# Edge scores by one matmul over two float parts, one-hots on ScalarE, and message weights in PSUM

## The chip, the cores and the metric

The kernel runs as one program on 1 core of one Trainium2 chip. The metric is the device time of an execution in microseconds (us); where kernels are compared, runs of both on the same chip are used.

## What is computed

A graph attention layer, a mixture of experts, a graph transformer layer and again a mixture of experts, over 2500 nodes with 256 features and 80000 edges that are sorted by destination. The part that matters here is in each graph layer. Layer 0 has H = 4 heads and no self loops, layer 1 has H = 8 heads and a self loop at every node.

```python
# layer 0 (H = 4): e_s and e_d are scores of nodes, h the nodes' values
scores = leaky_relu(e_s[src] + e_d[dst], 0.2)
m = segment_max(scores, dst)
ex = exp(scores - m[dst])
alpha = ex / segment_sum(ex, dst)[dst]
agg = segment_sum(alpha[:, :, None] * h[src], dst)
# layer 1 (H = 8): the same with one score s for both ends, Vh for h,
# and the edges (n, n) of the self loops added
```

## The kernel before

The 80000 edges are 640 tiles of 128 (`ET`); 8 tiles, 1024 edges, are an item (`ITEM`), so there are 80 items. In each graph layer `edge_layer` (L2110) runs three blocks one after the other, and a block ends when all engines have ended their part of it.

**The look-up**, `edge_scores` (L544), brings each edge the score of its source node. A node's number is split into a low part (100 values) and a high part (25 values). The scores lie in `keys` as 100 rows for the low part and 25 columns times H for the high part, and 25 further rows that hold a very negative number where the high part differs, so that a maximum over the 25 columns picks the right one. A one-hot of 125 rows (100 low, 25 high) by the 128 edges of a tile is PE's stationary operand. Float scores are cut into three bf16 parts by `split_scores` (L455), in `attention_features` and `transformer_features`, and three matmuls (L657) add them up in PSUM for each tile. The order is: SP loads the low numbers of an item, broadcast to 100 partitions (L599), ACT's queue the high numbers (L583), DVE compares with the partition's number (L614), PE does 24 matmuls (L657) into one of four PSUM lanes, and DVE takes the maximum (L620): once an item for H = 4, twice for H = 8. Ahead of it 44 matmuls with a shifted identity, `band` (L667, L669), move the scores from nodes' order into `keys` (L634).

At the same time POOL, in the same block, issues indirect DMAs of 128 rows each: 20 scatters (L568), then `gather_ahead` (L774), which gathers rows of messages (L795) and stores them in DRAM for later (L800): 160 gathers in layer 0 and 256 in layer 1. In layer 0 follow 24 early gathers into the ring (L756). The look-up on PE and DVE doesn't depend on them.

**The weights**, `edge_weights` (L812), turn scores into the softmax's shares, with scans over the sorted edges. This block isn't changed.

**The messages**, `pass_messages` (L964), are 176 steps of four tiles (`NS`, `GT`). POOL gathers rows of the source nodes into a ring (L756), SP reloads those gathered ahead (L1057) and reports rows as landed (L1063). In each step DVE makes the 0/1 matrix `pick` of edges by nodes (L1094), waits for the rows, multiplies them by the weights (`msg`, L1098), and adds the sum of two steps before, which lies in PSUM, to `acc` (L1107, `LATE = 2`). PE sums the edges of four tiles with f32 matmuls (L1121) into one of three PSUM banks (`DEPTH = 3`). In layer 1 ACT adds a tail of self-loop terms to `msg` (L1077). `staged` unrolls six steps in a loop. POOL may reuse a slot of the ring when `msg_ready` says that the multiply has read it.

`steps_of` (L105) writes the first `lanes` (4) items straight and the others as a loop of four items.

## Time and profile before

| what | value |
|---|---|
| median of 3 runs | 3143.92 us (3139.3 to 3148.53) |
| profiled execution | 3144.7 us, its span 3142.8 us |
| mean granted clock of PE | 0.764 |
| PE busy | 1798.8 us, 57% |
| DVE busy | 1769.9 us, 56% |
| POOL busy | 1701.8 us, 54% |
| ACT busy | 368.8 us, 12% |
| DMA | 361.01 MB, 115 GB/s |

No engine is busy for much over half of the span. The chain that ended last explains 5% of the span by itself, in the last stage, so that the reading has to go by stages. These are, from the timeline: look-up of layer 0 from 100 to 488 us, weights to 550, messages to 1203, experts to some 1590, look-up of layer 1 from 1600 to 2148, weights to 2279, messages from 2284 to 2817, the dense part and experts to the end.

### The profile page before, as it was taken

How to read it: one execution, taken by the hardware profiler on the slowest of the kernel's cores; microseconds unless marked ns; L12 is line 12 of the kernel's file. 1: busy time of each engine (PE TensorE's matmuls, PEld its weight loads, DVE VectorE, ACT ScalarE, POOL GpSimd, SP SyncE). 2: the span in 40 equal slices, each digit the busy share in tenths (PEclk: the TensorE clock that was granted, in tenths of full speed). 3: DMA queues.
4: the chain of work that ended last, by engine and by line, in shares of the span. 5: the costliest groups of instructions: out<-in, count | busy, mean ns of one | idle time of the engine just before them, and what ended most of it. 6: DMA issues, size and time to landing. Idle time of an engine off the chain costs nothing. (4 is left out here: it accounts for less than half of the span.)

```text
span 3142.8 us, 35335 instructions
## 1 busy us (share of the span) xinstructions
PE 1798.8 (57%) x10362; PEld 1444.4 (46%) x10362; DVE 1769.9 (56%) x2713; ACT 368.8 (12%) x715; POOL 1701.8 (54%) x1504
## 2 busy tenths in 40 slices
PE   2301292777755553999741112693177777756668
PEld 2200182555544442799740000693155555535557
DVE  6200098867644447455730000699787777757756
ACT  1100001000000001445200000000300000004244
POOL 3577606887877775000047777205878788761010
PEclk8655596888877776899865555797588888878889
DMA  3355553455433332000135566433145554430000
GB/s 121 119 190 189 173 184 95 126 160 162 136 92 92 92 91 74 1 1 0 63 89 196 196 200 198 148 117 112 54 146 165 162 165 162 134 115 8 4 31 34
DMA packets 140778, 361.01 MB, mean 115 GB/s; under 512 B 39352, under 2 KB 65360, under 8 KB 126890
## 3 DMA queue, kind: packets, MB, share of 16 engines
q0 software_dynamic: 69760, 225.91, 24.0%
q1 hardware_dynamic: 65866, 122.18, 11.2%
q10 hardware_dynamic: 5088, 12.13, 1.1%
q8 instruction: 32, 0.52, 0.1%
q14 instruction: 32, 0.26, 0.0%
HBM read 289.00 MB, written 71.12 MB: 115 GB/s over the span
## 5 line engine op out<-in xcount | busy, mean ns | idle before, releaser
L756 POOL DMA_INDIRECT e_ring<-table,e_index x840 | 1101.4, 1311 | 369.7 <-issue 255.5
L1121 PE MATMUL ms_ps_m<-ms_msg,ms_pick 128*128 128x260 f32 (+1 forms) x2816 | 830.4, 461 | 373.0 <-issue 258.2
L1121 PEld LDWEIGHTS ms_ps_m<-ms_msg,ms_pick 128*128 128x128 f32 x2816 | 634.4, 230 | 568.8 <-issue 432.3
L657 PE MATMUL sc_ps_e<-sc_keys,sc_hot 125*128 125x100 bf16 (+1 forms) x3840 | 353.7, 240 | 569.5 <-issue 561.3
L620 DVE TENSOR_REDUCE all_xn<-sc_ps_e 128x800 f32 (+1 forms) x240 | 234.1, 1019 | 633.7 <-remote 527.8
L657 PEld LDWEIGHTS sc_ps_e<-sc_keys,sc_hot 125*128 125x128 bf16 x3840 | 272.7, 102 | 650.3 <-issue 633.3
L795 POOL DMA_INDIRECT all_acc<-table,e_stage_index x416 | 397.1, 955 | 142.4 <-issue 141.1
L1098 DVE TENSOR_TENSOR ms_msg<-e_ring,all_xn 128x1040 f32 x176 | 218.0, 1239 | 254.1 <-SPq L1063 135.6
L1098 DVE TENSOR_TENSOR ms_msg<-e_ring,e_weight 128x1056 f32 x176 | 220.9, 1255 | 128.1 <-SPq L1063 112.7
L1094 DVE SCALAR_TENSOR_TENSOR ms_pick<-graph_dst_col,graph_tile_base,graph_lane_row 128x512 f32<-128x512 f32 x352 | 263.7, 749 | 12.0 <-issue 9.8
L1107 DVE TENSOR_TENSOR all_acc<-all_acc,ms_ps_m 128x260 f32 (+1 forms) x352 | 150.3, 427 | 8.3 <-PE ms_ps_m L1121 8.0
L131 POOL TENSOR_TENSOR w_qkv_low<-w_qkv,w_qkv_high 128x1536 fp32r<-128x1536 f32 x1 | 3.7, 3657 | 278.4 <-ACT w_qkv_high L126 278.4
L887 ACT ACTIVATE all_acc<-wt_ps_t 128x512 f32<-128x512 f32 x15 | 8.0, 624 | 1001.4 <-PE wt_ps_t L860 1001.3
L131 DVE TENSOR_TENSOR moe_hidden_low<-all_acc,moe_hidden_high 128x512 fp32r<-128x512 f32 x80 | 55.2, 692 | 94.7 <-ACT moe_hidden_high L126 94.7
L728 POOL COPY e_index<-graph_src_col 128x32 int32 (+1 forms) x40 | 14.4, 359 | 158.1 <-SPq L847 158.0
L1077 ACT ACTIVATE ms_msg<-e_dst_line 128x32 f32 x176 | 40.6, 231 | 499.8 <-PE ms_ps_m L1121 433.9
L140 PE MATMUL moe_ps_y<-moe_w_high,moe_hidden_high 128*128 128x256 f32 x320 | 91.4, 286 | 1.9 <-DVE moe_hidden_low L131 1.9
L140 PE MATMUL moe_ps_y<-moe_w_high,moe_hidden_low 128*128 128x256 f32 x320 | 91.6, 286 | 0.0
L140 PE MATMUL moe_ps_y<-moe_w_low,moe_hidden_high 128*128 128x256 f32 x320 | 91.5, 286 | 0.0
L419 ACT ACT_TABLE_LOAD x3 | 3.8, 1283 | 680.8 <-PEq L1142 670.8
L614 DVE TENSOR_SCALAR sc_hot<-sc_rows,all_node_of 125x1024 bf16<-125x1024 bf16 x160 | 80.7, 506 | 4.3 <-DMA sc_rows<-src_low 4.1
L446 PE MATMUL ln_ps_t<-all_ident,all_xn 128*128 128x128 f32 x160 | 31.2, 365 | 85.9 <-DVE all_xn L409 78.0
(415 smaller groups left out, 2682.0 us busy)
## 6 DMA issues: line engine op xcount, KB each, us to landing
ahead<-all_acc POOLq DMA_DIRECT2D x32, 1056.0 KB
e_ring<-ahead SPq DMA_DIRECT2D x32, 1056.0 KB
sc_rows<-src_low SPq DMA_DIRECT2D x160, 200.0 KB
ahead<-all_acc POOLq DMA_DIRECT2D x20, 1040.0 KB
e_ring<-ahead SPq DMA_DIRECT2D x20, 1040.0 KB
e_ring<-table,e_index POOLq DMA_INDIRECT x840
sc_rows<-src_high ACTq DMA_DIRECT2D x160, 50.0 KB
all_acc<-table,e_stage_index POOLq DMA_INDIRECT x416
```

Of the source, the lines that this page charges most:

```text
L131: return dve.tensor_tensor(low, value, high.bitcast(F32), ALU.subtract)
L140: product = pe.matmul(out, a, b, start=first and i == 0, stop=last and i == len(products) - 1)
L614: dve.tensor_scalar(hot[0:KEYS, q, :], rows[0:KEYS, q, :], s.node_of[0:KEYS, 0:1], None, ALU.is_equal).then_inc(hot_ready, 1)
L620: dve.tensor_reduce(edge[:, bass.ds(it * ITEM + sub * SL, SL), :], found, AX.X, ALU.max).then_inc(picked, 1)
L657: mm = pe.matmul(ps_e[lane][:, t * SLOT:t * SLOT + C], hot[0:KEYS, q, cols], keys[0:KEYS, part, :, :].rearrange("p g h -> p (g h)"), start ...
L756: pool.indirect_dma_start(out=g.ring[:, slot * QUAD + i // GT, i % GT, :], out_offset=None, in_=s.table[:, :], in_offset=bass.IndirectOffs ...
L795: pool.indirect_dma_start(out=stage.rows[:, b, t, :], out_offset=None, in_=s.table[:, :], in_offset=bass.IndirectOffsetOnAxis(ap=stage.ind ...
L1077: act.activation(msg[:, b, :, R:W], most[:, bass.ds(group * GT, GT), :], ACT.Copy).then_inc(tail_ready, 1)
L1094: dve.scalar_tensor_tensor(out=pick[:, b, :, :], in0=s.dst_col[:, bass.ds(group * GT, GT)].unsqueeze(2).broadcast_to([P, GT, P]), scalar=s ...
L1098: dve.tensor_tensor(msg[:, b, :, 0:R].rearrange("p t (h o) -> p t h o", h=H), ring[:, bass.ds(slot, 1), :, :].rearrange("p a t (h o) -> p ...
L1107: dve.tensor_tensor(into, into, ps_m[(b - LATE) % DEPTH][:, 0:W], ALU.add).then_inc(added, 1)
L1121: mm = pe.matmul(ps_m[b][:, 0:W], pick[:, b, t, :], msg[:, b, t, :], start=t == 0, stop=t == GT - 1)
```

## The change

In the look-up:

- `keys` holds two parts, both in TensorE's rounded float type (F32R): the score rounded to it, and what is left. They stand side by side, so that one matmul (L641) of 200 columns (H = 4) or 400 columns (H = 8) replaces three of 100 or 200. `split_scores` is gone; the band matmuls (L650, L652) take the float scores themselves and are f32.
- The one-hots are made by ScalarE with two operations: the distance from the partition's number (L590, `apart`, Abs) and then Relu of one minus it (L594, `hot`), in two buffers instead of four. The second waits until PE has looked up the item before last.
- PSUM is two lanes of four banks instead of four of two. DVE takes the maximum of both parts at once (L609, into `found`) and adds the two (L611), once an item for H = 4, twice for H = 8.
- Both loads of numbers (L573, L574) and that of `dst_line` are issued by SP.

In the messages:

- ACT copies the row 0..127 (`lane_row`) to PSUM (L1070), and for H = 4 all weights (L1072). For H = 8 ACT copies the weights of each step to one of three PSUM banks (L1067).
- DVE's `pick` (L1092) and `msg` (L1109) read these copies. The late add (L1101) now stands between the two, ahead of the wait for rows.
- The sums of a step use two banks instead of three.

```diff
+def edge_scores(nc, s, g, early, stage, tag, edge, keyed, node, node_dram, line, dst_line, dst_start, H):
 
     C = HI * H
-    SLOT = P if C <= P else 2 * P
-    SUBS = ITEM * SLOT // (2 * TB)
-    SL = ITEM // SUBS
-    BANK_HI = TB // (3 * H)
+    ROOM = 4 * TB
+    SLOT = TB // 2 if 2 * C <= TB // 2 else TB
+    SL = ROOM // SLOT
+    SUBS = ITEM // SL
...
         rows = m.sb("rows", [P, lanes, ITEM * P], BF16)
-        hot = m.sb("hot", [P, lanes, ITEM * P], BF16)
-        keys, band = m.sb("keys", [P, 3, HI, H], BF16), m.sb("band", [P, 3 * P], BF16)
-        ps_e = [m.ps(f"ps_e{i}", [P, 2 * TB]) for i in range(lanes)]
+        apart = m.sb("apart", [P, 2, ITEM * P], BF16)
+        hot = m.sb("hot", [P, 2, ITEM * P], F32R)
+        keys, band = m.sb("keys", [P, 2, H, HI], F32R), m.sb("band", [P, 3 * P])
+        found = m.sb("found", [P, 2, SL, 2, H])
+        ps_e = [m.ps(f"ps_e{i}", [P, ROOM]) for i in range(2)]
...
-            @block.scalar
...
-                    act.dma_start(rows[LOW:KEYS, q, :], s.src_high[bass.ds(it * (ITEM * P), ITEM * P)].partition_broadcast(HI)).then_inc(high_in[q], 16)
...
             @block.sync
             def _(sp):
                 def load(it, q, first):
                     if not first:
-                        sp.wait_ge(hot_ready, it - lanes + 1)
-                    sp.dma_start(rows[0:LOW, q, :], s.src_low[bass.ds(it * (ITEM * P), ITEM * P)].partition_broadcast(LOW)).then_inc(row_in[q], 16)
+                        sp.wait_ge(apart_ready, it - lanes + 1)
+                    edges = bass.ds(it * (ITEM * P), ITEM * P)
+                    sp.dma_start(rows[0:LOW, q, :], s.src_low[edges].partition_broadcast(LOW)).then_inc(row_in[q], 16)
+                    sp.dma_start(rows[LOW:KEYS, q, :], s.src_high[edges].partition_broadcast(HI)).then_inc(high_in[q], 16)
...
+            @block.scalar
+            def _(act):
+                def one_hot(it, q, first):
+                    act.wait_ge(row_in[q], (it - q) * (16 // lanes) + 16)
+                    act.wait_ge(high_in[q], (it - q) * (16 // lanes) + 16)
+                    act.activation(apart[0:KEYS, q % 2, :], rows[0:KEYS, q, :], ACT.Abs, scale=-1.0, bias=s.node_of[0:KEYS, 0:1]).then_inc(apart_ready, 1)
+                    if not first or q >= 2:
+                        act.wait_ge(looked, (it - 1) * SUBS)
+                    act.wait_ge(apart_ready, it + 1)
+                    act.activation(hot[0:KEYS, q % 2, :], apart[0:KEYS, q % 2, :], ACT.Relu, scale=-1.0, bias=1.0).then_inc(hot_ready, 1)
...
             @block.vector
             def _(dve):
-                def one_hot(it, q, first):
-                    dve.wait_ge(row_in[q], (it - q) * (16 // lanes) + 16)
-                    dve.wait_ge(high_in[q], (it - q) * (16 // lanes) + 16)
-                    if not first:
-                        dve.wait_ge(looked, (it - lanes + 1) * SUBS)
-                    dve.tensor_scalar(hot[0:KEYS, q, :], rows[0:KEYS, q, :], s.node_of[0:KEYS, 0:1], None, ALU.is_equal).then_inc(hot_ready, 1)
-
                 def select(it, q):
                     for sub in range(SUBS):
-                        dve.wait_ge(looked, it * SUBS + (sub + 1))
-                        found = ps_e[(q * SUBS + sub) % lanes][:, :].rearrange("p (t c) -> p t c", c=SLOT)[:, :, 0:C].rearrange("p t (g h) -> p t h g", h=H)
-                        dve.tensor_reduce(edge[:, bass.ds(it * ITEM + sub * SL, SL), :], found, AX.X, ALU.max).then_inc(picked, 1)
+                        turn, lane = it * SUBS + sub, (q * SUBS + sub) % 2
+                        dve.wait_ge(looked, turn + 1)
+                        sums = ps_e[lane][:, :].rearrange("p (t c) -> p t c", c=SLOT)[:, :, 0:2 * C].rearrange("p t (x g) -> p t x g", g=HI)
+                        dve.tensor_reduce(found[:, lane, :, :, :].rearrange("p t i h -> p t (i h)"), sums, AX.X, ALU.max).then_inc(picked, 1)
+                        dve.wait_ge(picked, turn + 1)
+                        dve.tensor_tensor(edge[:, bass.ds(it * ITEM + sub * SL, SL), :], found[:, lane, :, 0, :], found[:, lane, :, 1, :], ALU.add)
...
+                values = ps_e[0][0:LOW, 0:C].rearrange("p (g h) -> p h g", h=H)
+                dve.tensor_copy(keys[0:LOW, 0, :, :], values).then_inc(high_kept, 1)
+                dve.wait_ge(high_kept, 1)
+                low_part(dve, keys[0:LOW, 1, :, :], values, keys[0:LOW, 0, :, :]).then_inc(keys_ready, 1)
...
                 def look_up(it, q, first):
                     pe.wait_ge(hot_ready, it + 1)
                     for sub in range(SUBS):
-                        lane = (q * SUBS + sub) % lanes
-                        if not first or q * SUBS + sub >= lanes:
-                            pe.wait_ge(picked, it * SUBS + (sub + 1 - lanes))
+                        turn, lane = it * SUBS + sub, (q * SUBS + sub) % 2
+                        if not first or q * SUBS + sub >= 2:
+                            pe.wait_ge(picked, turn - 1)
                         for t in range(SL):
                             cols = slice((sub * SL + t) * P, (sub * SL + t + 1) * P)
-                            for part in range(3):
-                                mm = pe.matmul(ps_e[lane][:, t * SLOT:t * SLOT + C], hot[0:KEYS, q, cols], keys[0:KEYS, part, :, :].rearrange("p g h -> p (g h)"),
-                                               start=part == 0, stop=part == 2)
+                            mm = pe.matmul(ps_e[lane][:, t * SLOT:t * SLOT + 2 * C], hot[0:KEYS, q % 2, cols],
+                                           keys[0:KEYS, :, :, :].rearrange("p i h g -> p (i h g)"), start=True, stop=True)
                         mm.then_inc(looked, 1)
...
                 for hi in range(HI):
                     tile, skip = hi * LOW // P, hi * LOW % P
-                    at = hi // BANK_HI * TB + hi % BANK_HI * 3 * H
-                    into = ps_e[0][0:LOW, at:at + 3 * H].rearrange("p (i h) -> p i h", h=H)
+                    into = ps_e[0][0:LOW, hi * H:(hi + 1) * H]
                     over = skip + LOW > P
-                    mm = pe.matmul(into, band[:, P + skip:P + skip + LOW], parts[:, :, tile, :], start=True, stop=not over)
+                    mm = pe.matmul(into, band[:, P + skip:P + skip + LOW], keyed[:, tile, :], start=True, stop=not over)
                     if over:
-                        mm = pe.matmul(into, band[:, skip:skip + LOW], parts[:, :, tile + 1, :], start=False, stop=True)
+                        mm = pe.matmul(into, band[:, skip:skip + LOW], keyed[:, tile + 1, :], start=False, stop=True)
...
         pick = m.sb("pick", [P, DEPTH, GT, P])
         msg = m.sb("msg", [P, DEPTH, GT, W])
-        ps_m = [m.ps(f"ps_m{i}", [P, 512]) for i in range(DEPTH)]
+        BANKS = 2
+        ps_m = [m.ps(f"ps_m{i}", [P, 512]) for i in range(BANKS)]
+
+        ps_lane = m.ps("ps_lane", [P, 512])
+        lane_row = ps_lane[:, 0:P]
+        ps_w = m.ps("ps_w", [P, ET, H]) if most is None else [m.ps(f"ps_w{i}", [P, 512]) for i in range(DEPTH)]
...
+                    act.activation(ps_w[b][:, 0:GT * H].rearrange("p (t h) -> p t h", h=H), weight[:, bass.ds(group * GT, GT), :], ACT.Copy).then_inc(weight_set, 1)
                     act.activation(msg[:, b, :, R:W], most[:, bass.ds(group * GT, GT), :], ACT.Copy).then_inc(tail_ready, 1)
...
+                act.activation(lane_row, s.lane_row[:, :], ACT.Copy).then_inc(near_set, 1)
+                if most is None:
+                    act.activation(ps_w[:, :, :], weight[:, :, :], ACT.Copy).then_inc(weight_set, 1)
...
                         dve.scalar_tensor_tensor(out=pick[:, b, :, :], in0=s.dst_col[:, bass.ds(group * GT, GT)].unsqueeze(2).broadcast_to([P, GT, P]),
-                                                 scalar=s.tile_base[:, bass.ds(tile, 1)], in1=s.lane_row[:, :].unsqueeze(1).broadcast_to([P, GT, P]),
+                                                 scalar=s.tile_base[:, bass.ds(tile, 1)], in1=lane_row.unsqueeze(1).broadcast_to([P, GT, P]),
                                                  op0=ALU.subtract, op1=ALU.is_equal).then_inc(pick_ready, 1)
-                        dve.wait_ge(rows_landed, group + 1)
-                        dve.tensor_tensor(msg[:, b, :, 0:R].rearrange("p t (h o) -> p t h o", h=H),
-                                          ring[:, bass.ds(slot, 1), :, :].rearrange("p a t (h o) -> p (a t) h o", h=H),
-                                          weight[:, bass.ds(group * GT, GT), :].unsqueeze(3).broadcast_to([P, GT, H, O + 1]), ALU.mult).then_inc(msg_ready, 1)
                     if later(fixed, LATE):
 
                         dve.wait_ge(summed, n - (LATE - 1))
                         if later(fixed, LATE + 1):
                             dve.wait_ge(added, n - LATE)
                         into = acc[:, bass.ds(tile_late, 1), 0:W].rearrange("p a w -> p (a w)")
-                        dve.tensor_tensor(into, into, ps_m[(b - LATE) % DEPTH][:, 0:W], ALU.add).then_inc(added, 1)
+                        dve.tensor_tensor(into, into, ps_m[(q - LATE) % BANKS][:, 0:W], ALU.add).then_inc(added, 1)
+                    if fixed is None or fixed < NS:
+                        dve.wait_ge(rows_landed, group + 1)
+                        if most is None:
+                            shares = ps_w[:, bass.ds(group * GT, GT), :]
+                        else:
+                            dve.wait_ge(weight_set, n + 1)
+                            shares = ps_w[b][:, 0:GT * H].rearrange("p (t h) -> p t h", h=H)
+                        dve.tensor_tensor(msg[:, b, :, 0:R].rearrange("p t (h o) -> p t h o", h=H),
+                                          ring[:, bass.ds(slot, 1), :, :].rearrange("p a t (h o) -> p (a t) h o", h=H),
+                                          shares.unsqueeze(3).broadcast_to([P, GT, H, O + 1]), ALU.mult).then_inc(msg_ready, 1)
...
-                    if later(fixed, DEPTH):
-                        pe.wait_ge(added, n - (DEPTH - 1))
+                    if later(fixed, BANKS):
+                        pe.wait_ge(added, n - (BANKS - 1))
                     for t in range(GT):
-                        mm = pe.matmul(ps_m[b][:, 0:W], pick[:, b, t, :], msg[:, b, t, :], start=t == 0, stop=t == GT - 1)
+                        mm = pe.matmul(ps_m[q % BANKS][:, 0:W], pick[:, b, t, :], msg[:, b, t, :], start=t == 0, stop=t == GT - 1)
```

DVE in the message loop of layer 0, one step before (`graph_lane_row` is the row 0..127, `all_xn` holds the weights, ISA and REGISTER_ALU are waits and addresses):

```order
L1094 ISA
L1094 SCALAR_TENSOR_TENSOR ms_pick<-graph_dst_col,graph_tile_base,graph_lane_row 128x512
L1097 REGISTER_ALU
L1098 ISA
L1098 TENSOR_TENSOR ms_msg<-e_ring,all_xn 128x1040
L1107 ISA
L1107 TENSOR_TENSOR all_acc<-all_acc,ms_ps_m 128x260
```

and after (`ms_ps_lane` and `ms_ps_w` are the copies in PSUM):

```order
L1092 ISA
L1092 SCALAR_TENSOR_TENSOR ms_pick<-graph_dst_col,graph_tile_base,ms_ps_lane 128x512
L1101 ISA
L1101 TENSOR_TENSOR all_acc<-all_acc,ms_ps_m 128x260
L1103 REGISTER_ALU
L1109 ISA
L1109 TENSOR_TENSOR ms_msg<-e_ring,ms_ps_w 128x1040
```

The add of an earlier step has moved ahead of the multiply and its wait; the operations are the same three.

PE at the start of layer 0's look-up, the end of the band matmuls, the four items written straight, and the loop's first two of four items, before:

```order
L669 MATMUL sc_ps_e<-l_parts,sc_band 100x12
L657 MATMUL sc_ps_e<-sc_keys,sc_hot 128x100 x96
L108 UNCONDITIONAL_BRANCH
L108 ISA
L653 REGISTER_ALU
L657 MATMUL sc_ps_e<-sc_keys,sc_hot 128x100 x24
L649 REGISTER_ALU
L653 REGISTER_ALU
L657 MATMUL sc_ps_e<-sc_keys,sc_hot 128x100 x24
```

and after:

```order
L652 MATMUL sc_ps_e<-l_es,sc_band 100x4
L641 MATMUL sc_ps_e<-sc_keys,sc_hot 128x200 x32
L108 UNCONDITIONAL_BRANCH
L108 ISA
L638 REGISTER_ALU
L641 MATMUL sc_ps_e<-sc_keys,sc_hot 128x200 x8
L634 REGISTER_ALU
L641 MATMUL sc_ps_e<-sc_keys,sc_hot 128x200 x8
L634 REGISTER_ALU
L641 MATMUL sc_ps_e<-sc_keys,sc_hot 128x200 x8
```

An item is 8 matmuls instead of 24, and one pass of the loop 32 instead of 96.

ACT in layer 0's look-up loop, where before it only issued the load of `src_high`, after:

```order
L590 ACTIVATE sc_apart<-sc_rows,all_node_of 125x1024
L592 REGISTER_ALU
L593 REGISTER_ALU
L594 ACTIVATE sc_hot<-sc_apart 125x1024
L590 ACTIVATE sc_apart<-sc_rows,all_node_of 125x1024
L593 REGISTER_ALU
L594 ACTIVATE sc_hot<-sc_apart 125x1024
```

These two operations and their waits are new on ScalarE; DVE's one-hot (L614) is gone from its loop, where the reduction (L609) is followed by the add (L611).

## Rows read from the trace of the kernel before

**Rows 1.** Windows by stage: busy us (instructions) of PE, PEld, DVE, ACT, POOL; clock, DMA share, GB/s
```profile
100.00:390.00 290.00, 47.86 (x310) 28.24 (x311) 14.59 (x25) 0.00 (x0) 213.38 (x248) 0.51 0.54 172
390.00:488.00 98.00, 87.72 (x1655) 79.47 (x1655) 92.05 (x140) 0.00 (x0) 0.00 (x0) 0.95 0.53 181
552.00:1204.00 652.00, 427.92 (x1408) 333.86 (x1408) 388.19 (x532) 0.00 (x0) 517.23 (x431) 0.81 0.40 117
1600.00:1992.00 392.00, 72.66 (x286) 30.57 (x287) 23.08 (x36) 0.00 (x0) 290.27 (x342) 0.50 0.57 185
1992.00:2148.00 156.00, 153.58 (x1680) 142.40 (x1678) 155.78 (x212) 0.00 (x0) 0.00 (x0) 0.99 0.36 127
2284.00:2817.00 533.00, 402.52 (x1408) 300.56 (x1408) 393.67 (x529) 40.60 (x176) 421.92 (x325) 0.87 0.46 146
```

**Rows 2.** Groups of POOL, 552 to 1300 and 2290 to 2860: xcount | busy, mean ns | idle before, releasers
```profile
L756 POOL DMA_INDIRECT e_ring<-table,e_index x412 | 512.3, 1244 | 125.1 <-issue 124.4 <-DMA e_ring<-table,e_index 0.6
...
L756 POOL DMA_INDIRECT e_ring<-table,e_index x308 | 417.8, 1357 | 105.7 <-issue 94.9 <-DVE ms_msg L1098 10.5 <-DMA e_ring<-table,e_index 0.3
```

**Rows 3.** Timeline, message stage of layer 0: start, length, engine, operation [idle before]
```profile
698.51 6.60 PE L1121 MATMUL ms_ps_m<-ms_msg,ms_pick 128*128 128x260 f32 x28
...
699.45 1.24 DVE L1098 TENSOR_TENSOR ms_msg<-e_ring,all_xn 128x1040 f32 x1
699.66 1.85 POOL L756 DMA_INDIRECT e_ring<-table,e_index  x1 [0.30 <-issue]
...
703.96 0.94 POOL L756 DMA_INDIRECT e_ring<-table,e_index  x1 [0.30 <-issue]
```

**Rows 4.** Groups of DVE in the message stage of layer 0, 552 to 1203
```profile
L1098 DVE TENSOR_TENSOR ms_msg<-e_ring,all_xn 128x1040 f32 x176 | 218.0, 1239 | 254.1 <-SPq L1063 135.6 <-issue 118.5
L1094 DVE SCALAR_TENSOR_TENSOR ms_pick<-graph_dst_col,graph_tile_base,graph_lane_row 128x512 f32<-128x512 f32 x176 | 131.8, 749 | 5.9 <-issue 4.3 <-DVE all_acc L1085 0.8
L1107 DVE TENSOR_TENSOR all_acc<-all_acc,ms_ps_m 128x260 f32 x176 | 74.1, 421 | 3.2 <-PE ms_ps_m L1121 3.1
```

**Rows 5.** Groups of PE, 100 to 390
```profile
L657 PE MATMUL sc_ps_e<-sc_keys,sc_hot 125*128 125x100 bf16 x266 | 43.9, 262 | 240.9 <-issue 240.8
```

**Rows 6.** Timeline of DVE in the look-ups' first halves
```profile
310.57 0.99 DVE L620 TENSOR_REDUCE all_xn<-sc_ps_e 128x800 f32 x1 [57.54 <-remote]
...
1847.44 0.99 DVE L620 TENSOR_REDUCE all_xn<-sc_ps_e 128x800 f32 x1 [32.35 <-remote]
```

**Rows 7.** Timeline of all engines around POOL's pause at 355
```profile
355.08 0.58 POOL L800 DMA_DIRECT2D ahead<-all_acc  x1 [2.70 <-DMA all_acc<-table,e_stage_index]
...
355.73 5.65 PE L657 MATMUL sc_ps_e<-sc_keys,sc_hot 125*128 125x100 bf16 x66 [2.65 <-issue]
...
357.42 0.98 DVE L620 TENSOR_REDUCE all_xn<-sc_ps_e 128x800 f32 x1
357.97 0.95 POOL L756 DMA_INDIRECT e_ring<-table,e_index  x1 [0.30 <-issue]
```

**Rows 8.** Groups of DVE in the second half of layer 0, 390 to 487
```profile
L620 DVE TENSOR_REDUCE all_xn<-sc_ps_e 128x800 f32 (+1 forms) x71 | 70.1, 989 | 25.8 <-remote 25.4 <-PE sc_ps_e L657 0.3
L614 DVE TENSOR_SCALAR sc_hot<-sc_rows,all_node_of 125x1024 bf16<-125x1024 bf16 x68 | 32.9, 483 | 4.3 <-DMA sc_rows<-src_low 4.1
```

**Rows 9.** Groups of DVE by shape, whole span: one subtraction without and with PSUM
```profile
L131 DVE TENSOR_TENSOR moe_hidden_low<-all_acc,moe_hidden_high 128x512 fp32r<-128x512 f32 x80 | 55.2, 692 | 94.7 <-ACT moe_hidden_high L126 94.7
...
L131 DVE TENSOR_TENSOR w_xt_low<-ln_ps_t,w_xt_high 128x512 fp32r<-128x512 f32 x40 | 24.5, 688 | 10.2 <-issue 5.2 <-ACT w_xt_high L126 4.9
```

**Rows 10.** Groups of ACT by shape, whole span
```profile
L126 ACT ACTIVATE moe_hidden_high<-all_acc 128x512 fp32r<-128x512 f32 x80 | 50.6, 633 | 2.5
...
L126 ACT ACTIVATE exp_w_high<-exp_w 128x2048 fp32r<-128x2048 f32 x2 | 3.8, 1913 | 11.7 <-DMA exp_b<-L_ffn_b 7.8 <-DVEq L1809 4.0
```

**Rows 11.** Windows of line L657 alone: busy us (instructions) of PE and PEld; clock, DMA share, GB/s
```profile
100.00:211.00 111.00, 17.34 (x107) 9.64 (x108) 0.50 0.50 160
1600.00:1772.00 172.00, 28.46 (x107) 12.34 (x107) 0.51 0.53 170
```

100 lines of the change are left out of this document (39 added, 61 removed).

## The prediction

> **What bounds the kernel now.** I read the table of stretches first, because the share of busy time over 3142.8 us hides stages with different limits. It shows, for each graph layer, a look-up stage with two halves and a message stage [rows 1]. In the first half of each look-up POOL is busy for three quarters of the time with gathers, while PE and DVE do next to nothing. In the second half POOL is silent, PE and DVE are full, and nothing else runs. In the message stages POOL and PE are busy most of the time and DVE for 60 to 74%.
>
> Next, what ends the waits. In the message stages POOL's gathers take 1.244 and 1.357 us on average [rows 2]. The timeline shows why: a gather that starts during DVE's message multiply (L1098) lasts until shortly after it ends, 1.85 us; one that starts while DVE does not run takes 0.94 us, and 0.30 us of issue lie between two [rows 3]. So a free gather costs 1.25 us. The gather at 699.66 ends at 701.51, 0.82 us after the multiply ended at 700.69. DVE then waits for rows: 254.1 us of idle time stand before the multiply, 135.6 of them ended by SP's report that rows have landed [rows 4]. POOL's 412 gathers of layer 0 take 512.3 us and 125.1 between them, with 4 us of index copies 642 us; the 308 of layer 1 take 417.8 and 95, with the copies 517 us [rows 2]. POOL's gathers bound both message stages.
>
> In the look-up's first half PE is the late one: 266 matmuls in 290 us, 240.9 us of it idle with nothing that the profile shows [rows 5], the granted clock at 0.51 (1.2 GHz). DVE waits 57.54 us for one item of 1024 edges there [rows 6]. It is tied to POOL: when POOL pauses at 355 us for a store, PE does 66 matmuls in 5.65 us [rows 7]. I call this first half the storm. After it an item costs DVE one one-hot and one reduce, 0.483 + 0.989 less 0.17 of overlap (1.3 us), and in layer 1, with two reduces, 2.2 us: 71 items in 156 us [rows 1, 8].
>
> **Part 1: the message stages, -240 us.** Lane row and weights move to PSUM, so that pick and multiply each keep one SBUF input as the add (L1107) does already. If what stretches a gather is the second SBUF input, all of the stretch goes, and a gather costs 1.25 us throughout. Layer 0: 412 x 1.25 + 4 = 519 us instead of 642, **-123**. Layer 1: 308 x 1.25 + 4 = 389 instead of 517, -128; but DVE's own three ops take 2.41 us less 0.26 of overlap, 2.15 us a step [rows 4], 176 x 2.15 = 378, nearly as much, so they will wait for each other now and then: I take 11 us off, **-117**. The Trainium skill ("SBUF — State Buffer", section "Who interferes with whom") says that a VectorE instruction with two SBUF inputs holds a read interface that GpSimd's reads need, and with one it does not contend. By that rule the relief is full, as summed here. The trace agrees at both ends that it shows: the gather beside the two-input multiply waits it out, and one beside a reduce with no second input takes 0.95 us (357.97) [rows 7]; a multiply or pick with one operand in PSUM no row shows.
>
> Costs of this part. A PSUM operand: DVE's subtraction with one input from PSUM takes 688 ns against 692 from SBUF [rows 9], so nothing; the bound upwards is below, under the rivals. Filling PSUM with the weights, 2560 elements on ACT: 1.913 us for 2048 [rows 10] gives 2.4 us, beside DVE's and POOL's clearing of the accumulator, nothing. In layer 1 ACT, idle otherwise, makes one more copy of 32 elements a step, beside one that it makes now. The add now stands before the wait for rows and the multiply: with 2 banks instead of 3, PE's step n needs the add of n-2, which DVE issues in step n, ahead of that step's multiply. PE's 8 matmuls of a step take 1.9 us (28 of them ran in 6.60) [rows 3], below the 2.15 of DVE's step. Nothing, but with 0.25 us to spare.
>
> **Part 2: the look-up's second half, -122 us.** One matmul for 128 edges instead of three. PE's program shrinks too: one pass of the loop falls from 202 to 74 instructions (a matmul counts twice, weights and rows), the straight part ahead of it from 283 to 245, since each of the 44 band matmuls is now f32 and counts four times (the message matmuls show that: 8 rows for a step of 4). The question is what holds PE in the storm. It isn't the gathers as such: in the message stages PE runs 16 instructions each 2.15 us beside the same gathers, in a loop of 113. So I hold that long code, not each instruction, is slow there, and that a short loop runs free once it has been through one pass. Up to that point PE must issue 176 + 64 (four items) + 64 (the first pass) = 304 instructions. Before needed 88 for the band and 216 for 108 matmuls, 4.5 items, to get as far. PE's rows reach 108 at 211 us and at 1772 us [rows 11]; DVE's reduces end the fifth item at 311.6, with 58 us for it, so 4.5 items at 281, and the ninth half item of layer 1 at 1847 [rows 6]. I take the middles, 246 and 1810.
>
> From there 72 items are left at the slowest engine's pace. ACT: two ops of 1024 elements; 512 take 0.633 and 2048 1.913, 0.833 ns an element, so 1.06 each [rows 10], and a hand-off between them and PE: 2.35 us an item. DVE: the reduce of 1600 instead of 800 elements, 0.99 + 0.83 = 1.8, and 0.2 for the small add: 2.0 a turn; one turn an item in layer 0, two in layer 1, 4.0. PE: 8 matmuls of 200 or 400 columns in one pass each; 8 of 260 take 1.9 us, so 400 at most 2.9. Layer 0: 246 + 72 x 2.35 = 415 instead of 487, **-72**. Layer 1: 1810 + 72 x 4.0 = 2098 instead of 2148, **-50**.
>
> The page on ScalarE speaks against the one-hots' move: the Trainium skill ("ScalarE: Activation LUTs", section "Rules for kernel authors") wants relu-like work on VectorE, faster there per element. The rows bear it out, 2.1 us on ACT for what DVE does in 0.483. It would matter if the items had to run after the storm; then each costs 1.05 us more in layer 0 and 1.8 in layer 1 than now, and that is the first rival.
>
> Rest, at nothing: the split of scores (five DVE ops) goes, behind the table's write; both row loads on SP's queue instead of SP and ACT (two issues an item of 2.35 us, as long as they wait for nothing else); keys take two ops instead of one or two copies, 1 us.
>
> Sum: 3144.7 - 123 - 117 - 72 - 50 = 2783 against the profiled run; the median shown is 1 us lower. I forecast **2785 us**. Its own range: gathers at 1.20 to 1.35 (+-25), the short loop free from 211/1772 or 281/1847 (-35-38 or +35+37), ACT's item 2.2 to 2.6: 2690 to 2880.
>
> **Rivals.**
> *A. Each instruction stays slow in the storm.* Before's 266 matmuls in layer 0 [rows 5] and 286 - 44 = 242 in layer 1 [rows 1], less 44 for the second pass of the f32 band, are 222 and 198, at 8 an item 28 and 25 items. Left: 52 x 2.35 = 122 from 390, 512 (+25); 55 x 4.0 = 220 from 1992, 2212 (+64). 3144.7 - 240 + 89 = **2994**. For: 2.5 us between single matmuls looks like a per-instruction delay. Against: PE in the message stages. The Trainium skill ("Runtime: NRT & Kernel Launch", section "Instruction fetch mechanics") gives PE's instruction memory 2048 entries, filled in blocks of 256; both loops fit there, so by it their length should not decide, which speaks for this rival or B; that the storm delays PE at all no sentence there explains. Chance 0.27.
> *B. The look-up is never starved* and hides behind the gathers, ending with them at 390 and 1992: -97 - 156 - 240 gives **2652**. For: DVE's and ACT's work, 188 and 320 us, fits within the 290 and 392 us of storm. Against: the straight part of 245 instructions. 0.15.
> *C. The messages gain nothing* (what stretches a gather is DVE's being busy, not its second input), the look-up as forecast: 3144.7 - 122 = **3023**. For: the gather's tail of 0.82 us runs beside the add or pick. Against: the gather at 357.97, undisturbed by a reduce that had begun before it. 0.06.
> *D. Slower: operands from PSUM make pick and multiply longer*, because they are broadcast or strided there. The step is 1.239 + 0.749 + 0.421 less 0.26 of overlap, 2.15. With the look-up's -122 the kernel gets slower once the two message stages, 1185 us together, pass 1307, 3.71 us a step, which is 1.8 times on pick and multiply. At double, 4.14 us: 352 x 4.14 = 1457, +272, **3295**. Against: 688 beside 692 [rows 9], and the add's 0.42 us for 260 elements with PSUM. 0.04.
> No difference at all 0.02, other gains 0.06.
>
> **Numbers.** The forecast has 0.40. The range, 2640 to 3010, holds it with A and B. A change under 0.3% (9 us) can't be told from none here. Faster 0.94, same 0.02, slower 0.04 (D).
>
> **What would show it.** Right: the gathers' mean in the message stages near 0.955, DVE's multiply still 1.24; PE's look-up rows slow until about 246 and then 8 at a time each 2.35 us with POOL still gathering; the look-up's last reduce at 415 and, counted from its own start 1600, 498 us on in layer 1. A shows as single matmuls 2.5 us apart up to the last early gather; B as look-up items done by 300; C as gathers of 1.8 us beside DVE; D as longer L1092 and L1109. Wrong altogether: a message stage bound by DVE's waits on PE, or look-up items bound by SP's row loads.

## The result, and the profile after

The changed kernel takes 3401.4 us (median of 4 runs, 3357.75 to 3419.6), the kernel before 3142.86 beside it: the ratio is 1.0775, 95% interval 1.0671 to 1.0878. It is slower by 7.8% where 11% faster was forecast. (The ratio leaves out the slowest of the four executions, which lies over 1.5% above the fastest.) The profiled execution took 3357.75 us, its span is 3356.1, 213 us more than before.

Windows by stage of the changed kernel, columns as in [rows 1]: the look-up of layer 0 while POOL gathers and after it, the messages, and the same for layer 1. Layer 1's look-up begins at 1662 us in this trace, at 1600 before.

```profile
100.00:412.00 312.00, 123.12 (x516) 110.69 (x515) 105.87 (x109) 116.87 (x112) 211.41 (x247) 0.50 0.63 195
412.00:472.00 60.00, 53.58 (x216) 47.74 (x216) 54.15 (x58) 51.58 (x50) 0.95 (x1) 0.50 0.33 112
536.00:1266.00 730.00, 421.91 (x1407) 305.11 (x1408) 383.90 (x527) 0.00 (x0) 394.40 (x429) 0.78 0.35 104
1641.00:2055.00 414.00, 123.55 (x432) 94.18 (x430) 121.36 (x154) 59.82 (x57) 289.48 (x341) 0.52 0.59 189
2055.00:2286.00 231.00, 175.98 (x428) 120.54 (x429) 210.48 (x218) 108.41 (x104) 0.82 (x3) 0.53 0.20 69
2423.00:3032.00 609.00, 412.61 (x1408) 290.63 (x1408) 390.61 (x532) 61.39 (x352) 296.33 (x325) 0.84 0.40 126
```

By the instructions of each stage on DVE (us; a difference is against before; a look-up ends with the end of its last reduce):

| | before | forecast | after |
|---|---|---|---|
| look-up of layer 0 ends, and the first multiply comes | 487, 555 | -72 | 470, 537 (-18) |
| messages of layer 0, from first to last multiply | 642 | -123 | 726 (+84) |
| from there to the end of layer 1's look-up | 949 | -50 | 1019 (+70) |
| messages of layer 1 | 524 | -117 | 602 (+78) |

The rest makes -1. Of the 949 us before, layer 1's look-up took 548 (1600 to 2148); now it takes 622 (1662 to 2284), 74 more. Both message stages, which were to give 240 us, cost 162. Groups of the changed kernel in the message stage of layer 0, DVE's and then POOL's; they answer to [rows 4] and [rows 2]:

```profile
L1109 DVE TENSOR_TENSOR ms_msg<-e_ring,ms_ps_w 128x1040 f32 x176 | 216.5, 1230 | 0.0
L1092 DVE SCALAR_TENSOR_TENSOR ms_pick<-graph_dst_col,graph_tile_base,ms_ps_lane 128x512 f32<-128x512 f32 x176 | 130.5, 742 | 0.8 <-DVE all_acc L1079 0.8
L1101 DVE TENSOR_TENSOR all_acc<-all_acc,ms_ps_m 128x260 f32 x175 | 73.8, 422 | 344.4 <-remote 281.0 <-PE ms_ps_m L1126 55.4 <-issue 8.0
...
L739 POOL DMA_INDIRECT e_ring<-table,e_index x412 | 391.2, 950 | 294.3 <-DVE ms_msg L1109 171.2 <-issue 122.6 <-DMA e_ring<-table,e_index 0.3
```

The first step of the forecast came true: a gather takes 0.950 us on average instead of 1.244, the multiply 1.230 and the pick 0.742, so operands in PSUM cost nothing here. POOL isn't late any more, it waits 171 us for DVE. DVE no longer waits for rows (0.0 before the multiply) but 344 us ahead of its add, for the sum of two steps earlier.

What it waits for is PE, though PE's rows don't show it. A timeline of layer 1's messages, DVE, ACT and PE; ACT's copy L1067 and DVE's add L1101 wait for no other engine than PE, by the count of sums that it has finished:

```profile
2596.66 3.25 PE L1126 MATMUL ms_ps_m<-ms_msg,ms_pick 128*128 128x272 f32 x12
2599.72 1.25 DVE L1109 TENSOR_TENSOR ms_msg<-e_ring,ms_ps_w 128x1056 f32<-128x1056 f32 x1
2600.88 0.74 DVE L1092 SCALAR_TENSOR_TENSOR ms_pick<-graph_dst_col,graph_tile_base,ms_ps_lane 128x512 f32<-128x512 f32 x1
2601.16 2.10 PE L1126 MATMUL ms_ps_m<-ms_msg,ms_pick 128*128 128x272 f32 x8 [1.25 <-issue]
2612.77 0.20 ACT L1067 ACTIVATE ms_ps_w<-e_weight 128x32 f32 x1 [13.15 <-DMA sc_rows<-src_low]
2612.78 0.44 DVE L1101 TENSOR_TENSOR all_acc<-all_acc,ms_ps_m 128x272 f32 x1 [11.15 <-DMA sc_rows<-src_low]
```

The last matmuls have their rows at 2601.16. The add needs the step before those, whose rows end at 2599.91, and both engines go on together only at 2612.77, 12.9 us later. (The ends of PE's rows are modelled; their starts are recorded.) (The DMA named there used the same semaphore earlier; "remote" is the same wait in layer 0.) POOL issued gathers without a break from 2592.04 and its last at 2610.87, 2 us before:

```profile
2592.04 0.98 POOL L739 DMA_INDIRECT e_ring<-table,e_index  x1 [11.78 <-DVE ms_msg L1109]
...
2610.87 0.95 POOL L739 DMA_INDIRECT e_ring<-table,e_index  x1 [0.30 <-issue]
```

DVE and ACT do nothing in these 11 us, so it isn't their reading or writing of PSUM that holds PE there. Counted over both layers, the 221 adds that have a gather in their wait or in the 1 us before it carry 537 us of waits, the 131 others 27. (POOL gathers for most of these stages, so this fits and doesn't prove.)

The look-up shows it too. Timeline of DVE in layer 0: it waits 108 us for the band matmuls, whose recorded rows end at 125, and 19 us for an item whose matmuls are among the 16 rows from 207.94 to 211.68.

```profile
207.32 0.26 DVE L622 CAST sc_keys<-sc_ps_e 100x100 fp32r<-100x100 f32 x1 [108.45 <-issue]
207.62 0.26 DVE L131 TENSOR_TENSOR sc_keys<-sc_ps_e,sc_keys 100x100 fp32r<-100x100 f32 x1
226.87 1.82 DVE L609 TENSOR_REDUCE sc_found<-sc_ps_e 128x64 f32<-128x1600 f32 x1 [18.99 <-remote]
```

From 251 to 380 items pass every 2.7 us on average beside the gathers, as forecast from 246. In layer 1 turns pass every 2.17 us from 1828 to 1893, and then the same loop falls back to some 9 us a turn until POOL is done at 2054:

```profile
1893.26 1.82 DVE L609 TENSOR_REDUCE sc_found<-sc_ps_e 128x64 f32<-128x1600 f32 x1
1895.23 0.19 DVE L611 TENSOR_TENSOR all_xn<-sc_found 128x32 f32 x1 [0.15 <-issue]
1901.01 1.82 DVE L609 TENSOR_REDUCE sc_found<-sc_ps_e 128x64 f32<-128x1600 f32 x1 [5.58 <-remote]
```

So the same loop runs free beside gathers at one time and not at another. The windows of layer 0, slow and then free, and for comparison the third from e13, whose look-up is the same code:

```profile
130.00:250.00 120.00, 7.74 (x32) 7.06 (x32) 4.56 (x6) 4.19 (x4) 88.56 (x106) 0.50 0.56 183
251.00:355.00 104.00, 74.25 (x296) 65.92 (x296) 74.20 (x75) 78.42 (x75) 67.46 (x80) 0.50 0.84 254
```

```profile
251.00:349.00 98.00, 12.07 (x48) 10.70 (x48) 12.10 (x12) 12.57 (x12) 75.23 (x90) 0.50 0.65 212
```

In e4, e11 and e13 the loop of layer 0 isn't freed at all: 6 items from 251 to 349, where this trace has 35 from 251 to 355. POOL gets somewhat fewer instructions done where PE is free (80 in 104 us against 106 in 120 and 90 in 98); which of the two is the cause these traces don't tell.

**Theory S** of the experiments: where gathers follow each other every 1.25 us, PE finishes its matmuls late, and freeing POOL in the message stages let it do so. **Its first rival, O**: the new order of DVE and the two banks cost the time. Below, "waits" are DVE's before the add of layer 0 and layer 1, "messages" the first to the last multiply of each. e5, e6, e8, e10, e12 and e13 are single executions, so small differences of theirs tell nothing.

### The profile page after: what moved, and what is told of

Read it like the earlier page. It is cut to its first block and busy times, and to the rows that moved or that the text cites. A ratio compares the mean times of both kernels' runs of the same rounds, so it can differ in the third digit from the quotient of the medians.

```text
span 3356.1 us, 31184 instructions
## 1 busy us (share of the span) xinstructions
PE 1899.8 (57%) x7890; PEld 1482.8 (44%) x7890; DVE 1954.1 (58%) x2784; ACT 727.7 (22%) x1214; POOL 1453.4 (43%) x1504
## 5 line engine op out<-in xcount | busy, mean ns | idle before, releaser
L739 POOL DMA_INDIRECT e_ring<-table,e_index x840 | 854.8, 1018 | 678.0 <-DVE ms_msg L1109 359.4
L1126 PEld LDWEIGHTS ms_ps_m<-ms_msg,ms_pick 128*128 128x128 f32 x2816 | 595.9, 221 | 767.2 <-issue 653.5
L641 PE MATMUL sc_ps_e<-sc_keys,sc_hot 125*128 125x200 f32 (+1 forms) x1280 | 428.0, 498 | 504.0 <-issue 256.9
L641 PEld LDWEIGHTS sc_ps_e<-sc_keys,sc_hot 125*128 125x128 f32 x1280 | 325.6, 322 | 607.6 <-issue 295.0
L609 DVE TENSOR_REDUCE sc_found<-sc_ps_e 128x64 f32<-128x1600 f32 x240 | 437.8, 1824 | 262.7 <-remote 216.1
L1101 DVE TENSOR_TENSOR all_acc<-all_acc,ms_ps_m 128x260 f32 (+1 forms) x352 | 150.6, 428 | 563.7 <-remote 281.0
L1109 DVE TENSOR_TENSOR ms_msg<-e_ring,ms_ps_w 128x1040 f32 (+1 forms) x352 | 436.1, 1239 | 0.4 <-ACT ms_ps_w L1067 0.4
L594 ACT ACTIVATE sc_hot<-sc_apart 125x1024 fp32r<-125x1024 bf16 x160 | 169.1, 1057 | 632.5 <-remote 464.4
L1092 DVE SCALAR_TENSOR_TENSOR ms_pick<-graph_dst_col,graph_tile_base,ms_ps_lane 128x512 f32<-128x512 f32 x352 | 261.0, 741 | 0.8 <-DVE all_acc L1079 0.8
L590 ACT ACTIVATE sc_apart<-sc_rows,all_node_of 125x1024 bf16<-125x1024 bf16 x160 | 181.3, 1133 | 73.2 <-DMA sc_rows<-src_high 71.7
L1067 ACT ACTIVATE ms_ps_w<-e_weight 128x32 f32 x176 | 35.4, 201 | 547.3 <-PE ms_ps_m L1126 301.7
L1325 ACT ACTIVATE all_acc<-moe_ps_h,moe_bias 128x512 f32<-128x512 f32 x80 | 55.1, 689 | 118.3 <-PE moe_ps_h L140 117.6
```

Source lines behind the costliest of these rows:

```text
L590: act.activation(apart[0:KEYS, q % 2, :], rows[0:KEYS, q, :], ACT.Abs, scale=-1.0, bias=s.node_of[0:KEYS, 0:1]).then_inc(apart_ready, 1)
L594: act.activation(hot[0:KEYS, q % 2, :], apart[0:KEYS, q % 2, :], ACT.Relu, scale=-1.0, bias=1.0).then_inc(hot_ready, 1)
L609: dve.tensor_reduce(found[:, lane, :, :, :].rearrange("p t i h -> p t (i h)"), sums, AX.X, ALU.max).then_inc(picked, 1)
L641: mm = pe.matmul(ps_e[lane][:, t * SLOT:t * SLOT + 2 * C], hot[0:KEYS, q % 2, cols], keys[0:KEYS, :, :, :].rearrange("p i h g -> p (i h g) ...
L739: pool.indirect_dma_start(out=g.ring[:, slot * QUAD + i // GT, i % GT, :], out_offset=None, in_=s.table[:, :], in_offset=bass.IndirectOffs ...
L1092: dve.scalar_tensor_tensor(out=pick[:, b, :, :], in0=s.dst_col[:, bass.ds(group * GT, GT)].unsqueeze(2).broadcast_to([P, GT, P]), scalar=s ...
```

## The experiments

**e1**, only the look-up: `pass_messages` as before. 

> The look-up as changed, the messages as before. Theory S (PE's matmuls finish late while POOL's gathers follow each other every 1.25 us, and the PSUM operands free POOL to do so in the message stages): the message stages are as before, 648 and 533 us, and only the look-up's share is left, about -18 us in layer 0 and +94 in layer 1 as read in the changed kernel: about 3220 us. Rival O (DVE's new order and two banks make the message stages slow, independent of POOL): the same here. Either is wrong if this kernel is above 3300.

Measured 3265.67 us, ratio 1.040 (1.031 to 1.049); messages 641 and 527, as before. 131 us of the loss are the look-up's, half of it, and more than expected (3220).

**e2**, only the messages: `edge_scores` and what feeds it as before. 

> The messages as changed, the look-up as before. Both theories: the message stages take about 713 and 610 us instead of 648 and 533, about 3285 us in all. A result under 3150 would say that the loss needs both parts.

3279.11 us, 1.046 (1.040 to 1.051); messages 715 and 601. 144 us; with e1's 131 that is 275, near the 259 of both together.

**e3**, e2 with DVE's old order:

```diff
-                    (late add)
                     if fixed is None or fixed < NS:
                         dve.wait_ge(rows_landed, group + 1)
                         (multiply)
+                    (late add)
```

> As e2, with DVE's order of before (pick, wait for rows, multiply, then the late add), two banks and the operands in PSUM. Theory S: PE still finishes late, so the wait only moves; message stages within 30 us of e2's, 3250 to 3300 us. Rival O: the loss is gone and the freed gathers show, message stages 519 and 400 us, about 2905 to 2950.

3290.33 us, 1.052 (1.047 to 1.058); messages 708 and 604. DVE's add in layer 0:

```profile
L1128 DVE TENSOR_TENSOR all_acc<-all_acc,ms_ps_m 128x260 f32 x176 | 74.7, 424 | 306.8 <-remote 285.2 <-issue 11.4 <-PE ms_ps_m L1143 9.8
```

The wait stays where it was, ahead of the add, though the multiply now stands before it. So the order isn't the cause. The two banks, the other half of O, are in this run too; against them speaks e8 below, on a chip where the same two banks and the new order leave 32 us of waits. Three banks with the operands in PSUM weren't run.

**e4**, the gathers of the messages further apart:

```diff
             pool.indirect_dma_start(out=g.ring[...
+            for _ in range(4):
+                pool.sem_inc(gap, 1)
```

> The changed kernel with four increments of a semaphore behind each gather of the message stages, so that gathers follow each other at longer distance than 1.25 us (about 1.45 to 1.6). Theory S: DVE's waits for PE ahead of the add shrink from some 280 us to under 80 a stage, the message stages get shorter although POOL issues slower, by 40 to 100 us each: 3220 to 3320. Rival O: POOL isn't what the stage waits for, so the same time as the changed kernel, 3358 to 3420, or longer.

3334.97 us (3250.92 to 3378.88), too spread for a ratio. Its profile: messages 670 and 574, waits 289 and 188. POOL's row gives the mean distance, 0.946 + 178.7/412 = 1.38 us:

```profile
L739 POOL DMA_INDIRECT e_ring<-table,e_index x412 | 389.9, 946 | 242.1 <-issue 178.7 <-DVE ms_msg L1113 63.3
```

But the mean hides how it comes about: of the 395 gaps in "issue" 322 are still at most 0.35 us long, and 46 of over 0.6 us make 68 us. Most gathers are as close as before, with pauses among them. The stages got shorter by 56 and 28 us, as S has it; the waits stayed far above the 80 us that it asked for. For an even distance of 1.38 us this is no test.

**e5 to e8** ran on another chip, and that changed the question: there the kernel before took 2937.26 us, not 3135.

**e5**, narrow rows in the messages (`0:g.piece` of the ring, 20 or 22 of 260 or 264 numbers). 

> The changed kernel, but the gathers of the message stages that follow the ring's first filling take 80 or 88 bytes of each row instead of 1040 or 1056 (the messages are then other values; the rest is computed as before). The number of gather instructions, their pace and their descriptors are the same, the bytes are a twelfth. Theory S1 (PE finishes late because of the bytes that the gathers move): DVE's waits before the add fall below 60 us a stage, message stages 519 and 400 us. Theory S2 (because of the gather instructions or their descriptors): the waits stay at 280 us and 200 us, stages above 680 and 560.

2686.01 us; messages 520 and 399, waits 30 and 8.

**e6**, `pick` and `msg` declared in F32R. 

> The changed kernel with pick and messages in the rounded float type, so that PE has 4 matmuls of one pass in a step instead of 8 rows (the sums then lose bits). Theory S with a fixed price for each of PE's instructions while gathers run: half of them, so DVE's waits before the add halve, to about 150 and 110 us, message stages near 560 and 480. If it is the length of a stall and not a price of an instruction: no change, 726 and 602.

2680.37 us; messages 522 and 400, waits 1 and 1.

**e7**, the kernel before with `lane_row` in PSUM alone. 

> The kernel before with only the row 0..127 moved to PSUM: the pick has one SBUF input, the multiply still two, so a gather is still held for 1.24 us of each step. Theory S: PE keeps the breathing space of the multiply; gathers get a little faster (those held by the pick), message stages 0 to 60 us shorter each if the gathers' 1.85 us fall, 3040 to 3145 us. If the held gathers were not what saves PE, waits ahead of the add appear as in the changed kernel, over 3180 us.

2932.55 us, 0.998 (0.997 to 1.000); messages 637 and 523. The pick alone holds hardly any gather: POOL's mean is 1.232 us, against 1.235 in e17, whose messages are unaltered, on the same chip.

**e8**, in the look-up:

```diff
+                pool.wait_ge(looked, NITEM * SUBS)
                 gather_ahead(pool, s, stage)
```

> The changed kernel, but POOL starts the gathers of the look-up stage only when all items are looked up. Theory S: nothing holds PE, an item takes 2.1 to 2.4 us in layer 0 and 4.2 in layer 1, so the first reduce comes by 112 and some 18 us after the stage begins, the look-up takes 190 and 345 us, and the gathers follow with 215 and 350. If PE is late for a reason of its own (the f32 band, 176 instructions, the two waits on ScalarE), the band still ends some 100 us late, and items take more than 3 and 5 us.

3104.39 us; the look-up's last reduce begins at 282, 170 us after the first at 112, and in layer 1 338 us after the first. But its message stages, which are the changed kernel's word for word, took 521 and 400 us instead of 726 and 602, with this add:

```profile
L1102 DVE TENSOR_TENSOR all_acc<-all_acc,ms_ps_m 128x260 f32 x176 | 78.7, 447 | 32.1 <-PE ms_ps_m L1127 32.0
```

So e5 and e6 tell nothing of bytes or instructions; PE isn't late on this chip. In e7's trace even the look-up of the kernel before (its edit touches the messages alone) ends at 264 us, not 487. Here are its end and the end of the same look-up on a chip like the first (e10):

```profile
263.46 0.99 DVE L620 TENSOR_REDUCE all_xn<-sc_ps_e 128x32 f32<-128x800 f32 x1 [0.48 <-PE sc_ps_e L657]
```

```profile
485.47 2.78 DVE L620 TENSOR_REDUCE all_xn<-sc_ps_e 128x800 f32 x3
```

**e9**, the changed kernel again. 

> The changed kernel, unaltered. e5 to e8 ran on another chip (number 0) than e1 to e4 (number 13); there the kernel before took 2937 us, not 3135, and the message stages of the changed kernel, which e8 left as they are, took 521 and 400 us instead of 726 and 602, with hardly a wait for PE. Theory C (PE's lateness under the gathers belongs to the chip, or to its condition at the time, and the kernels only meet it): on a chip where the kernel before takes about 2937 us this one takes about 2685, as e6; where before takes about 3135, about 3400. Theory S as first stated (the kernel alone decides): 3358 to 3420 anywhere.

Once more beside a before of 3136.47 us: 3378.22, 1.077 (1.071 to 1.083), messages 724 and 606, waits 344 and 223.

**e10**, the kernel before again. 

> The kernel before, unaltered, for its profile on this chip. Theory C: either the look-up of layer 0 ends near 263 us behind which POOL's gathers end at 390 (the free chip), or near 485 us (the chip on which PE is late). Theory S: 485 us on any.

3133.76 us; the look-ups end at 488 and 2143. So the kernel before is late on this chip as well, and theory C holds: the chip, or its condition, has a part in it.

**e11**, e6 again, now where PE is late. 

> As e6, the changed kernel with pick and messages in the rounded float type. On a chip where PE isn't late: the same as the changed kernel within 10 us, since DVE's waits for PE are 30 us there and POOL bounds the stage. On a chip where PE is late: half of PE's instructions, so message stages near 620 and 500 instead of 726 and 602, about 3200 us.

3280.38 us (3216.4 to 3338.15, too spread for a ratio) beside e9's 3378.22; messages 643 and 560. Its add and its pick in layer 0, with half of PE's instructions:

```profile
L1101 DVE TENSOR_TENSOR all_acc<-all_acc,ms_ps_m 128x260 f32 x176 | 75.1, 427 | 208.5 <-remote 188.0 <-issue 14.8 <-PE ms_ps_m L1126 5.4
L1092 DVE SCALAR_TENSOR_TENSOR ms_pick<-graph_dst_col,graph_tile_base,ms_ps_lane 128x512 fp32r<-128x512 f32 x176 | 131.9, 749 | 53.2 <-issue 51.0 <-remote 1.2 <-DVE all_acc L1079 0.8
```

Before the add DVE waits 208 and 49 us instead of 344 and 223. But part of the wait has only moved: 53 and 61 us stand before the pick, where e9 has 1 and 0, and in layer 1 64 before the multiply. All of DVE's waits together are 263 and 174 us against 345 and 223, which is what the stages gained (81 and 46). So half of PE's instructions take a quarter off the lateness, not half. PE's busy time fell by half as well (417 to 213 us in layer 0), so the two aren't told apart.

**e12**, e1 again. 

> As e1, the look-up as changed and the messages as before. Where PE isn't late: the look-up hides behind POOL's gathers with either form of it, so the same as the kernel before within 15 us. Where PE is late: 3266 us against 3135 as in e1.

3145.68 us beside 3136, where e1 lost 131. Its look-ups end at 472 and 2156, against 494 and 2262 in e1. Nor is it the chip alone that decides: from the last multiply of layer 0 to the end of layer 1's look-up e12 takes 978 us, and e9, on the same chip with the same look-up, 1049. The look-up's share of the loss changes between executions, with how long the loop runs free. Neither expectation held.

**e13**, e5 again, where PE is late (before: 3139.19). 

> As e5 (after the ring's first filling the gathers of the message stages take 80 or 88 bytes a row; the messages are then other values), to be read on a chip where PE is late. Bytes: if the gathers' traffic is what holds PE, DVE's waits before the add fall from 344 and 223 us to under 80, message stages 520 and 400 us. Instructions or descriptors: the waits stay over 250 and 150 us, stages over 650 and 540. If the kernel before takes about 2937 us beside it, the chip is a free one and nothing is learnt beyond e5.

3451.1 us; messages 723 and 607. The gathers' traffic in 600 us of the stage falls from 46.70 MB to 3.67, and the wait is unchanged:

```profile
L1105 DVE TENSOR_TENSOR all_acc<-all_acc,ms_ps_m 128x260 f32 x176 | 74.2, 421 | 341.9 <-remote 251.2 <-PE ms_ps_m L1130 63.0 <-issue 27.5
```

The gathers' queue in the changed kernel and then in e13, packets, MB and share:

```profile
q0 software_dynamic: 16837, 46.70, 27.9%
```

```profile
q0 software_dynamic: 11392, 3.67, 5.9%
```

Bytes and bandwidth are out; what remains are the gather instructions (350 and 355 in these windows) and their descriptors. The packets that the profile counts fell by a third and took nothing off the wait.

**e14**, the kernel before, its look-up's gathers spaced by twelve increments as in e4. 

> The kernel before with twelve increments of a semaphore behind each gather of gather_ahead (160 and 256 of them), so that these follow each other every 1.65 us or so instead of 1.25; nothing else changed. Theory S (back-to-back gathers make PE late): PE gets through more items beside the gathers, the look-up's first half is longer by 64 and 100 us, the second shorter or gone: look-ups end near 450 and 2080 instead of 485 and 2140. If PE's lateness doesn't depend on the gathers' distance: PE keeps its pace of some 2.5 us a matmul, does 25% more in the longer first half, and the look-ups end 40 to 90 us later than before.

3048.94 us on the same chip as e13, ratio 0.971 (0.968 to 0.975). POOL's row, and the window until the look-up's last reduce at 295 (it ends at 296 instead of 487):

```profile
L796 POOL DMA_INDIRECT all_acc<-table,e_stage_index x160 | 153.6, 960 | 109.9 <-issue 91.4 <-DMA ahead<-all_acc 17.8 <-POOL e_stage_index L782 0.8
```

```profile
100.00:295.00 195.00, 126.97 (x1964) 111.38 (x1964) 109.52 (x162) 0.00 (x0) 110.20 (x124) 0.81 0.71 217
```

91.4 us over 152 gaps are 0.60 us each, so a gather every 1.56 us on average; the median gap is 0.45, and 44 are still 0.35 or less. PE does 1964 matmuls in 195 us there, where it did 310 in 290 [rows 1]. PE doesn't only use POOL's longer pauses: in the 36 stretches of 1.3 to 1.5 us from one start on POOL to the next, 50 us in all, 628 matmuls start. This is the plainest support of S, stronger than it asked for: 0.30 us more between gathers, on average, gives PE back nearly all, and the kernel before is 90 us faster for it. It holds for the look-up; and what the distance does and what the increments themselves do isn't told apart.

**e15 to e18** met a chip on which PE isn't late (before: 2935.46 us), so they tell what the change is worth there, not where the threshold lies.

**e15**, the changed kernel, twelve increments everywhere. 

> The changed kernel with twelve increments behind every gather, in the look-up and in the messages (e14 measured 0.60 us between gathers with them instead of 0.30, so 1.56 us from one to the next). Theory S: PE isn't late any more. DVE's waits before the add fall below 60 us a stage, gathers bound the stages again: 412 x 1.56 + 4 = 647 and 308 x 1.56 + 4 = 484 us; the look-ups end before the gathers do. In all near e14, 3049, less 40 in layer 1's messages: about 3010 us. If the distance helped only beside the look-up's instructions, the message stages stay over 680 and 570 and the time over 3120.

2979.49 us, 1.015 (1.013 to 1.017); messages 640 and 503: bound by the distance, 0.946 + 235.5/412 = 1.52 us on average. Here the increments only cost.

**e16**, eight increments. 

> The same with eight increments (about 1.50 us from one gather to the next). Theory S with a threshold above 1.38 us (e4 left 289 and 188 us of waits) and not above 1.56: either still free, stages 620 and 466, look-up stages 10 and 15 us shorter than with twelve, about 2950 us; or PE late in part, over 3050.

2702.15 us, **0.920 (0.919 to 0.922)**; messages 522 and 416.

```profile
L1107 DVE TENSOR_TENSOR all_acc<-all_acc,ms_ps_m 128x260 f32 x176 | 76.5, 435 | 31.3 <-PE ms_ps_m L1132 31.2
```

```profile
L740 POOL DMA_INDIRECT e_ring<-table,e_index x412 | 390.1, 947 | 125.0 <-issue 122.7 <-DVE ms_msg L1115 2.1
```

On this chip eight increments don't widen the gap at all (122.7/412 = 0.30 us), so this is the changed kernel itself, within little. (Unaltered it never ran on this chip.)

**e17**, the kernel before, six increments in the look-up. 

> The kernel before with six increments in gather_ahead instead of e14's twelve (about 1.44 us). The look-up's first reduces tell how far PE is late at this distance: if the threshold lies below 1.44, look-ups end near 300 and 1790 as in e14 and the kernel takes 3020 to 3035 us; if above, look-up ends lie between those and 485 and 2140, and the time between 3050 and 3140.

2940.79 us, 1.002 (1.001 to 1.003): no gain where PE isn't late, and six increments hardly widen a gap here either.

**e18**, F32R messages, eight and four increments. 

> The changed kernel with pick and messages in the rounded float type (half of PE's instructions), eight increments behind the gathers of the look-up and four behind those of the messages (1.38 us). Theory S: with half of the instructions PE keeps up at the shorter distance; waits before the add below 60 us, stages 412 x 1.38 + 4 = 573 and 429 us, about 2890 us and the fastest of all on such a chip. If half isn't enough at 1.38 us: stages above 620 and 500, about 3000.

2682.7 us, **0.915 (0.913 to 0.917)**; messages 521 and 398. As fast as e6 without increments (2680.37 us on the same chip).

## Why the prediction was wrong, step by step

- **What bounds the message stages**: right. The gathers did, and DVE's two-input multiply stretched them. With PSUM operands they take 0.950 us.
- **Part 1, -240 us**: on the chip of the forecast +162; on the free chip 639 and 524 (e17) against 522 and 416 (e16), which is -225, and the whole kernel gains 8%. The term was sized well and taken for granted where it doesn't hold. The step that failed stands in part 2: "It isn't the gathers as such: in the message stages PE runs 16 instructions each 2.15 us beside the same gathers". They were not the same. The multiply held each of them for up to 1.24 us in 2.15, 1.55 us from one to the next on average; freed, they are the storm that the forecast had seen in the look-up and never carried over. What the runs show in its place: DVE waits 344 and 218 us for PE's sums, and the stages take 726 and 602 us instead of 519 and 407. In the look-up e14 has PE recovered at 1.56 us on average; where between 1.25 and 1.56 it sets in, e4 with its uneven gaps doesn't say, and for the messages no run does.
- **Part 2, "long code, not each instruction, is slow there, and a short loop runs free once it has been through one pass"**: wrong. The loop did run free from 251, beside the 246 of the forecast, but in layer 1 the same loop fell back (1895 to 2054), in e4, e11 and e13 layer 0's never ran free beside the gathers, and e14 shows the long loop of 202 instructions running free. The right first date was luck. Layer 0 gave -18 for -72: 49 items were done by 380, and then two by 407. Layer 1's look-up gave +74 for -50.
- **ACT's and DVE's pace**: near. An item took 2.1 us in e8's look-up and 2.3 in e16's (forecast 2.35), a turn of DVE 2.1 (2.0).
- **The rivals**: A (0.27) came nearest, with PE slow at each instruction for as long as the gathers last, but only for the look-up, so its 2994 is as wrong; and its even price doesn't hold either, as the loop freed from 251 to 380 shows. C and D didn't happen; D had the sign with another mechanism. B is what the free chip does: look-ups end long before the gathers, so they give nothing there. No rival had PE as the one who pays in the message stages; "a message stage bound by DVE's waits on PE" stood last in the text, with no price.
- **Not settled**: why a gather makes PE late at all, and why on some chips only. The runs fell on chips numbered 13, 10 and 5 (before: 3134 to 3139 us) and 0, twice (2937 and 2935); each kept its kind in all its runs. Why the same loop beside the same gathers is free for 70 or 130 us and then late again stays open too, so S names what the lateness needs and not all that decides it. The message stage at a distance of 1.56 us wasn't measured on a chip of the first kind, nor e18.

## What to carry to other kernels

An engine that is held up shields others: before freeing it, ask who has only been spared, and look for a stage of the same trace where it already runs free, here POOL in the look-up, to see what it does to its neighbours. A wait for an engine whose rows have ended is still a wait for that engine; two other engines released at the same instant tell it. And a verdict of some per cent may belong to the chip: compare on more than one before a change is kept or dropped. Where PE is late beside gathers, 0.3 us more between those of the look-up, on average, were worth 2.9% without any other edit (e14); on the chip where it isn't late, increments gained nothing. And a wait that shrinks before one instruction may stand before another: add up all of an engine's waits in the stage, and look at the single gaps behind a mean.
